# Turning the context of a cross-attention kernel on VectorE in 32x32 squares instead of on TensorE

## The reference

```
q = x @ Wq; k = ctx @ Wk; v = ctx @ Wv          # per head, 32 channels each
p = softmax(q @ k.T / sqrt(32))
out = merge_heads(p @ v) @ Wo + bias + x
```

## Time and profile before

| | |
|---|---|
| median of three runs | 1901.07 us |
| profiled execution | 1897.36 us, of which the span is 1895.7 us |
| TensorE busy | 1828.4 us (96%) |
| VectorE busy | 1184.8 us (63%) |
| ScalarE busy | 1044.8 us (55%) |
| GpSimd busy | 690.8 us (36%) |
| first phase, to TensorE's last matmul | about 316 us |
| second phase, from VectorE's first instruction | 326.4 us to the end |

### The profile page before, as it was taken

One profiled execution on the slowest core, in us unless ns is written; L12 is line 12 of the kernel. 1 busy time (PEld: TensorE's weight loads), 2 busy tenths in 40 slices (PEclk: granted clock), 3 DMA queues, 4 the chain that ended last, 5 costly groups with the idle time before them and its releaser, 6 DMA issues.

```text
span 1895.7 us, 41902 instructions
## 1 busy us (share of the span) xinstructions
PE 1828.4 (96%) x14960; PEld 1498.5 (79%) x14960; DVE 1184.8 (63%) x2402; ACT 1044.8 (55%) x5597; POOL 690.8 (36%) x865
## 2 busy tenths in 40 slices
PE   8999996789999999999999999999999999999998
PEld 7999996567777777777777777777777777777777
DVE  3201001677777777777777777777777777777762
ACT  4312111566666666666666666666666666666661
POOL 1111111244444444444444444444444444444441
PEclk9999998899999999999999999999999999999998
DMA  7522111688888888888888888888888888888873
GB/s 257 153 69 86 58 44 45 165 221 228 243 243 241 242 242 243 242 240 245 235 243 244 235 247 239 242 237 236 239 241 240 245 243 241 239 245 244 242 212 131
DMA packets 271397, 399.36 MB, mean 211 GB/s; under 512 B 41088, under 2 KB 119024, under 8 KB 271200
## 3 DMA queue, kind: packets, MB, share of 16 engines
q1 hardware_dynamic: 183008, 301.62, 54.2%
q10 hardware_dynamic: 83904, 82.59, 17.6%
q0 software_dynamic: 4288, 12.62, 1.9%
HBM read 216.37 MB, written 180.39 MB: 209 GB/s over the span
## 4 chain that ended last, share of the span: by engine, by line
PE 45%; DMA 22%; DVE 6%; ACT 5%; SPq 2%; issue 1%; POOL 1%; ACTq 0%; DVEq 0%
PE p_bank L776 21%; DMA p_scratch<-turned 15%; PE p_bank L735 14%; DMA probs_t<-p_scratch 7%; PE p_scores L750 5%; PE p_bank L762 5%; ACT probs L595 5%; DVE negmax L638 2%; SPq L508 2%; DVE turned L654 2%; DVE x_t L676 1%; POOL probs L562 1%; DVE x_bias L684 0%; DVE q_t L661 0%; DVE o_t L665 0%
## 5 line engine op out<-in xcount | busy, mean ns | idle before, releaser
L595 ACT ACTIVATE probs<-p_scores,negmax 128x77 f32<-128x77 f32 x2560 | 788.0, 362 | 550.4 <-DVE negmax L638 550.4
L562 POOL TENSOR_TENSOR probs<-probs,rsum 128x308 f32<-128x308 f32 x640 | 446.7, 700 | 895.6 <-DVE rsum L644 895.4
L776 PEld LDWEIGHTS p_bank<-wo_split,o_t 128*128 128x128 f32 x3840 | 567.6, 189 | 134.5 <-issue 131.3
L595 ACT ACTIVATION_READ_ACCUMULATOR probs<-p_scores,negmax 128x1 f32 x2560 | 624.5, 244 | 0.0
L776 PE MATMUL p_bank<-wo_split,o_t 128*128 128x320 f32 x3840 | 616.5, 315 | 0.6 <-DVE x_bias L684 0.6
L735 PE MATMUL p_bank<-x_t,wq_split 128*128 128x512 f32 x2400 | 597.1, 401 | 15.9 <-DVE x_t L676 15.9
L735 PEld LDWEIGHTS p_bank<-x_t,wq_split 128*128 128x128 f32 x2400 | 444.7, 190 | 115.4 <-DVE x_t L676 17.1
L654 DVE STREAM_TRANSPOSE turned<-probs 128x384 f32<-128x384 f32 x640 | 356.5, 557 | 29.2 <-POOL probs L562 28.8
L638 DVE TENSOR_REDUCE negmax<-p_scores 128x16 f32<-128x1232 f32 x160 | 229.3, 1433 | 48.0 <-PE p_scores L750 46.6
L644 DVE RECIPROCAL rsum<-sums 128x4 f32<-128x4 f32 x640 | 110.7, 173 | 178.6 <-ACT probs L595 174.1
L762 PE MATMUL p_bank<-probs_t,v_sb 77*32 77x512 f32 x1280 | 172.0, 609 | 26.9 <-DMA probs_t<-p_scratch 23.0
(11 more groups left out here) (28 smaller groups left out, 626.4 us busy)
## 6 DMA issues: line engine op xcount, KB each, us to landing
p_scratch<-turned SPq DMA_DIRECT2D x160, 768.0 KB, 6.8
probs_t<-p_scratch SPq DMA_DIRECT2D x320, 256.0 KB
x_bias<-in_x ACTq DMA_DIRECT2D x128, 320.0 KB, 3.7
out<-x_bias SPq DMA_DIRECT2D x128, 320.0 KB, 5.6
x_raw<-in_x ACTq DMA_DIRECT2D x124, 320.0 KB, 5.2
probs_t<-p_scratch SPq DMA_DIRECT2D x160, 104.0 KB
ctx_raw<-in_ctx SPq DMA_DIRECT2D x19, 512.0 KB, 4.7
k_sb<-k_scratch SPq DMA_DIRECT2D x32, 192.5 KB, 6.2
```

What stands on the lines that cost most here:

```text
L562: nc.gpsimd.tensor_tensor(heads_of(t), heads_of(t), rsum[:, slot, t, :].unsqueeze(2).to_broadcast([P, HG, N_TXT]), ALU.mult).then_inc(prob ...
L595: last = nc.scalar.activation(heads_of(t)[:, h, :], s_bank[:, h, t * N_TXT:(t + 1) * N_TXT], ACT.Exp, bias=negmax[:, slot, t, h:h + 1], ac ...
L776: last = nc.tensor.matmul(to_bank[:, 0:HALF], o_t[parity][:, o, c, t * P:(t + 1) * P], wo_s[:, w, c, hf * HALF:(hf + 1) * HALF], start=c = ...
```

## The change

The context is no longer turned by TensorE. SyncE loads a block in four transfers, one for each quarter of the channels (L189 of the new file): partition i * 32 + q of `ctx_raw` holds, for each of the eight groups n of 32 tokens, the 256 channels of quarter i of token n * 32 + q. Runs in memory are 256 floats instead of 1024. All four count on one semaphore for each half.

VectorE then transposes squares of 32x32 inside each group of 32 partitions (L292), 512 columns an instruction, into a new SBUF tile `ctx_turned` with two slots. ScalarE and VectorE read that in place of the PSUM bank for the high part (L251) and the low part (L298). The channels come out in another order: chunk k has channels i * 256 + k * 32 + s on partition i * 32 + s. Therefore the rows of wk and wv are loaded in that order too, by one transfer of a rearranged view for each chunk, and wq now likewise. The identity, its semaphores and two PSUM banks go.

`blocks` is a Python loop over all ten blocks; no engine has a hardware loop any more. `attend` is unchanged.

```diff
+CK = CA // (P // SQ)
...
-def blocks(eng, body):
-
-    for j in range(HEAD):
-        body(j, j % 2)
-    with eng.Fori(0, PAIRS) as i:
-        for half in range(2):
-            body(2 * i + (HEAD + half), (HEAD + half) % 2)
-    for j in TAIL:
+def blocks(body):
+
+    for j in range(BLOCKS):
         body(j, j % 2)
...
-            "ident": sbuf("ident", [P, P]),
-
...
-        ctx_raw = sbuf("ctx_raw", [P, CSLOTS, CA])
+        ctx_raw = sbuf("ctx_raw", [P, 2, TB // SQ, CK])
+        ctx_turned = sbuf("ctx_turned", [P, 2, 2, TB])
...
-        bank = [stack.enter_context(nc.psum_tensor(f"p1_bank{i}", [P, 512], F32)) for i in range(6)]
-        t_bank, k_bank, v_bank = bank[0:2], bank[2:4], bank[4:6]
-
-        id_zero, id_ready = sem("id_zero"), sem("id_ready")
+        bank = [stack.enter_context(nc.psum_tensor(f"p1_bank{i}", [P, 512], F32)) for i in range(4)]
+        k_bank, v_bank = bank[0:2], bank[2:4]
...
+        ctx_v = ctx.rearrange("(n q) (i c) -> i q n c", q=SQ, i=P // SQ)
...
-            def load_block(j, parity):
-                for i, (t0, rows) in enumerate(tiles_of(tokens_of(j))):
-                    slot = parity * CTILES + i
-                    if not isinstance(j, int) or j >= 2:
-
-                        sp.wait_ge(t_done, TU * (j - 1))
-                    sp.dma_start(ctx_raw[0:rows, slot, :], ctx[bass.ds(j * TB + t0, rows), :])\
-                      .then_inc(c_loaded[slot], DMA)
-
-            load_block(0, 0)
+            def load_block(j):
+                if j >= 2:
+                    sp.wait_ge(t_turned, TU * (j - 1))
+                n0, n1 = j * TB // SQ, (j * TB + tokens_of(j)) // SQ
+                for i in range(P // SQ):
+                    sp.dma_start(ctx_raw[i * SQ:(i + 1) * SQ, j % 2, 0:n1 - n0, :], ctx_v[i][:, n0:n1, :])\
+                      .then_inc(c_loaded[j % 2], DMA)
+
+            load_block(0)
             for n, (dram, _, k) in enumerate(chunks):
                 if n >= WSLOTS:
                     sp.wait_ge(w_split, n - WSLOTS + 1)
-                if dram is wq:
-                    for i in range(P // SQ):
-                        r = i * CQ + k * SQ
-                        sp.dma_start(stage[i * SQ:(i + 1) * SQ, n % WSLOTS, :], dram[r:r + SQ, :])\
-                          .then_inc(w_loaded[n % WSLOTS], DMA)
-                else:
-                    sp.dma_start(stage[:, n % WSLOTS, :], dram[k * P:(k + 1) * P, :])\
-                      .then_inc(w_loaded[n % WSLOTS], DMA)
+                rows = (dram[k * P:(k + 1) * P, :] if dram is wo else
+                        dram.rearrange("(i k s) c -> k i s c", i=P // SQ, s=SQ)[k])
+                sp.dma_start(stage[:, n % WSLOTS, :], rows).then_inc(w_loaded[n % WSLOTS], DMA)
...
@@ ScalarE
             def context_high(j, parity, u):
...
-                act.wait_ge(t_done, TU * j + u + 1)
+                act.wait_ge(t_turned, TU * j + u + 1)
                 nc.scalar.activation(ctx_t[parity][:, 0, 2 * u:2 * u + 2, 0:tokens],
-                                     t_bank[u % 2][:, 0:2 * tokens].rearrange("p (k t) -> p k t", k=2),
-                                     ACT.Copy).then_inc(t_high, 1)
+                                     ctx_turned[:, u % 2, :, 0:tokens], ACT.Copy).then_inc(t_high, 1)
...
@@ VectorE
+            def turn_context(j, parity, u):
+                n = tokens_of(j) // SQ
+                if u == 0:
+                    dve.wait_ge(c_loaded[parity], DMA * (P // SQ) * (j // 2 + 1))
+                if TU * j + u >= 2:
+                    dve.wait_ge(t_split, TU * j + u - 1)
+                blocks_in = ctx_raw[:, parity, 0:n, 2 * u * SQ:2 * (u + 1) * SQ]
+                nc.vector.transpose(ctx_turned[:, u % 2, :, 0:n * SQ].rearrange("p k (n q) -> p k n q", q=SQ),
+                                    blocks_in.rearrange("p n (k q) -> p k n q", q=SQ)).then_inc(t_turned, 1)
+
...
+            turn_context(0, 0, 0)
             for u in range(TU):
+                if u + 1 < TU:
+                    turn_context(0, 0, u + 1)
                 context_low(0, 0, u)
             split_weights(range(WK_CHUNKS))
 
             def body(j, parity):
                 for m in range(CC):
-                    if m < TU and not (isinstance(j, int) and j == BLOCKS - 1):
+                    if m < TU and j < BLOCKS - 1:
+                        turn_context(j + 1, 1 - parity, m)
                         context_low(j + 1, 1 - parity, m)
                     split_weights(splits_at(j, m))
...
@@ TensorE
-            def transposes(j, parity, u):
-                tokens = tokens_of(j)
-                if not isinstance(j, int) or TU * j + u >= 2:
-                    pe.wait_ge(t_split, TU * j + u - 1)
...
-            pe.wait_ge(id_ready, 1)
-            for u in range(TU):
-                transposes(0, 0, u)
-
             def body(j, parity):
                 for m in range(CC):
                     keys(j, parity, m)
-                    if m < TU and not (isinstance(j, int) and j == BLOCKS - 1):
-                        transposes(j + 1, 1 - parity, m)
                 values(j, parity)
```

More of the change, by code:

```diff
@@ L165, in loads_by @@
         def loads_by(n):
-            return sum(P // SQ if chunks[i][0] is wq else 1 for i in range(n % WSLOTS, n + 1, WSLOTS))
+            return n // WSLOTS + 1
+        ctx_v = ctx.rearrange("(n q) (i c) -> i q n c", q=SQ, i=P // SQ)
         def splits_at(j, m):
-            if not isinstance(j, int) or j >= HEAD:
+            if j >= HEAD:
                 return range(0)
@@ L220, in _ @@
                 sp.dma_start(kept["x_raw"][i * SQ:(i + 1) * SQ, 0, :, :], x_v[0][i]).then_inc(x_loaded, DMA)
-            with sp.Fori(0, PAIRS - 1) as i:
-                for half in range(2):
-                    load_block(2 * i + (4 + half), half)
-            for j in TAIL:
-                load_block(j, j % 2)
+            for j in range(4, BLOCKS):
+                load_block(j)
         @block.gpsimd
         def _(pool):
-            nc.gpsimd.memset(ident[:, :], 0.0).then_inc(id_zero, 1)
-            pool.wait_ge(id_zero, 1)
-            nc.gpsimd.affine_select(out=ident[:, :], in_=ident[:, :], compare_op=ALU.not_equal, fill=1.0,
-                                    base=0, pattern=[[-1, P]], channel_multiplier=1).then_inc(id_ready, 1)
             def store(j, parity):
@@ L270, in keys_out @@
                 act.wait_ge(k_done, CC * j + m + 1)
-                if not (isinstance(j, int) and CC * j + m < 2):
+                if not (CC * j + m < 2):
                     act.wait_ge(k_stored[slot], DMA // 2 * (CC * j + m - slot))
@@ L279, in values @@
                     act.wait_ge(v_done, VU * j + u + 1)
-                    if not (isinstance(j, int) and j == 0 and u < 2):
+                    if not (j == 0 and u < 2):
                         act.wait_ge(v_stored[u % 2], DMA * (VU // 2 * j + u // 2))
@@ L291, in body @@
                     keys_out(j, parity, m)
-                    if m < TU and not (isinstance(j, int) and j == BLOCKS - 1):
+                    if m < TU and not (j == BLOCKS - 1):
                         context_high(j + 1, 1 - parity, m)
@@ L295, in body @@
                 values(j)
-            blocks(act, body)
+            blocks(body)
         @block.vector
@@ L321, in body @@
                 for m in range(CC):
-                    if m < TU and not (isinstance(j, int) and j == BLOCKS - 1):
+                    if m < TU and j < BLOCKS - 1:
+                        turn_context(j + 1, 1 - parity, m)
                         context_low(j + 1, 1 - parity, m)
                     split_weights(splits_at(j, m))
-            blocks(dve, body)
+            blocks(body)
         @block.tensor
         def _(pe):
-            def transposes(j, parity, u):
-                tokens = tokens_of(j)
-                if not isinstance(j, int) or TU * j + u >= 2:
-                    pe.wait_ge(t_split, TU * j + u - 1)
-                for i, (t0, rows) in enumerate(tiles_of(tokens)):
-                    slot = parity * CTILES + i
-                    if u == 0:
-                        pe.wait_ge(c_loaded[slot], DMA // 2 * (j - parity) + DMA)
-                    for k in range(2):
-                        last = nc.tensor.transpose(t_bank[u % 2][:, k * tokens + t0:k * tokens + t0 + rows],
-                                                   ctx_raw[0:rows, slot, (2 * u + k) * P:(2 * u + k + 1) * P],
-                                                   ident[0:rows, 0:rows])
-                last.then_inc(t_done, 1)
             def keys(j, parity, m):
                 slot, tokens = (parity * CC + m) % 2, tokens_of(j)
-                if not (isinstance(j, int) and CC * j + m < 2):
+                if not (CC * j + m < 2):
                     pe.wait_ge(k_copied, CC * j + m - 1)
@@ L382, in body @@
                     keys(j, parity, m)
-                    if m < TU and not (isinstance(j, int) and j == BLOCKS - 1):
```

(3 more changed lines are left out.)

28 lines of the change are left out of this document (12 added, 16 removed).

## The result

The changed kernel takes 1932.46 us in the median (1930.7 to 1934.56, 4 runs), the kernel before 1900.92 (1899.89 to 1902.59, 4 runs): ratio 1.0165, 95% interval 1.0148 to 1.0183. It is 31.5 us slower where I forecast 10.3 us faster, and lies far outside the range. The profiled execution took 1934.56 us, its span is 1932.7.

A forecast was written before the change was run, and what follows sets the result against it. TensorE was taken to bound the first phase; -10.1 and -2.3 (transposes), +1.2 (start), +0.7 (block 0) and +0.2 (clock) sum to -10.3 us, so 1901.07 becomes 1890.8 us, range 1887.0 to 1897.0.

The forecast's parts named there:

- the sentence on the weights' loads: Start: weight loads of 320 KB, queued behind the context, land ahead of their use; no cost in the sum.
- Transposes, 12.4 us: TensorE, first phase: removing transposes saves 1.44 us in each of blocks 1 to 7 and 2.3 in block 8.
- Rival D: First phase: TensorE's matmuls don't close up where transposes stood, blocks stay at 30.2 us; 1903.2 us, 4%.
- Loops, 0: First phase: loop registers and branch cost TensorE nothing, so unrolling gains 0.
- Start, +1.2 us: Start: context lands at 7.0 us, then turns; first weight subtraction at 12.5 instead of 11.29 us.
- Rival A: Start: the context comes at full rate and the start costs next to nothing; -11.4 us, 1889.7 us, 15%.
- My line between rates by run length: Context load: between 640-byte and 4096-byte runs, 1024 bytes cost 56 ns, giving 291 GB/s and 3.6 us.
- the prediction's 3.4 us: Start: time by which the context load of before landed above its pure transfer time, carried over to the new load.
- Block 0's pace on VectorE, +0.7 us: Block 0: VectorE's order sets a 3.53 us period, TensorE waits 2.2 us; +0.7 instead of a 1.4 gain.
- the +0.2 for the clock: Start: TensorE's clock stays at 1.2 GHz a little past unit 0, so unit 1 pays; 0 to +0.5 us.
- Rival B: Block 0 or start: TensorE's wait or late start lowers its clock; +2.7 to +5.4, 1893.5 to 1896.2 us, 12%.
- Rival C: Second phase: moved addresses and timing add waits for probabilities through memory; 23 us longer, 1913.8 us, 6%; sign over 1572 us.

The follow-up runs named there:

- e1: Changed kernel with each weight chunk loaded as one plain piece of 128 rows, permutation left out; 1891.9 us, ratio 0.9964.
- e2: Changed kernel with the weight rows of a chunk taken in eight pieces of 16 rows, not matching the context's channels; 1909.2 us, ratio 1.0064.
- e4: Kernel before with only wk and wv loaded by the rearranged view in four pieces; 1939.9 us, ratio 1.0216.
- e8: Kernel before with the first phase written out without hardware loops, nothing else changed; 1900.2 us, ratio 1.0005.
- e5: Changed kernel with the same permuted weight rows, each chunk loaded by four transfers of 32 rows; 1896.4 us, ratio 0.9983.
- e6: Changed kernel with permuted wk and wv loaded by quarters of the channels, four chunks a transfer, wq by four transfers a chunk; 1903.1 us, ratio 1.0013.
- e12: Changed kernel with wk and wv rows at a stride of 8 over 128 partitions, VectorE's turns strided and one unit ahead, wq by four transfers; 1890.0 us, ratio 0.9949.
- e10: e1 with VectorE turning the context one unit ahead, in front of the weight subtractions; 1887.4 us, ratio 0.9939.
- e11: Changed kernel, turns one unit ahead, each wk and wv chunk in four 32-row transfers over the queues of SyncE, ScalarE and GpSimd; 1897.3 us, ratio 0.9989.
- e9: e6 with VectorE's turns one unit ahead and the identity's memory allocated again, unused; 1899.5 us, ratio 0.9998 to the kernel before.

## Why the prediction was wrong

**The step that failed** is the sentence on the weights' loads: "needed one in 0.75 us; they land one in 0.8 us from about 8 us on, ahead of their use". I took the rate of plain loads for the rearranged view. The view has four pieces outermost, runs on 4 of 16 engines, and lands a chunk in 3.19 us; that moved the start of the second phase by 39.3 us (e1), where the sum had nothing for it. The prediction named this load no further and had no rival for it: all my care with rates went to the context, where the order of instructions showed another shape, while `128x1x640` for the weights looked like the old `128x640`. The diff did show it: a slice of "(i k s) c -> k i s c" cannot be one dimension of 128. e1, e2 and e4 show the cause: 39 us in the changed kernel, 41 in the kernel before, halved engines and rates in step with the number of pieces.

**Transposes, 12.4 us**: right, a little small; 14.7 were won (7 x 1.73 + 2.6 in block 8). Rival D fell with that. A block lasts 28.47 us, not 28.76, since 120 matmuls in one piece run at 0.120 us each and not 0.1225: 1.73 a block instead of 1.44. The 390 ns for a transpose that the prediction quotes from the Trainium skill, "VectorE: DVE Perf Modes", section "The three transpose paths", stand there for bf16, and the context here is float32.

**Loops, 0**: right (e8).

**Start, +1.2 us**: the mechanism was right, the size small. VectorE begins at 7.73, not 7.0, and TensorE at 14.10 instead of 12.17, +1.9. Rival A, with a landing at 5.9, fell. From the landing to the first weight subtraction it is 5.49 us (7.73 to 13.22) where I had 5.5. My line between rates by run length was the wrong law: context (1024 bytes) at 223 to 234 GB/s in the changed kernel, x (640) at 218 to 251, weights (2560) in quarters at 241 in e5 are all alike and all go to 32 partitions a transfer. (The stages of x hold some other traffic too: of the 1.26 MB between 66.5 and 71.5 us 0.16 are stores, of the 1.31 between 329.5 and 335.5 us 0.47 came through another queue than x.) What the three have in common is the partitions, and the cleanest pair is e6 and e1, 225 against 394 GB/s from 10 to 12 us; e12 shows that the order of the rows in memory isn't it, since rows 8 apart come at 394. No run tried a number of partitions between 32 and 128. The Trainium skill, "SBUF — State Buffer", section "Door 1: The DMA port swizzle", says that 32 partitions reach 8 of 16 ports, about 218 GB/s. By it 1.05 MB take 4.8 us and, with the prediction's 3.4 us on top, land at 8.2, an estimate from that figure; they landed at 7.73. The stages measured here lie between 203 and 261 GB/s, so some are above it. By the rule that the prediction cites, 512 bytes for line rate in the Trainium skill, "DMA: Bandwidth & Descriptors", section "Specifications", runs of 1024 bytes would have come at full rate; they came at 223 to 234, so it is not what set the rate here.

**Block 0's pace on VectorE, +0.7 us**: the mechanism was right. The period was forecast at 3.53 and is 3.51, TensorE's wait 2.2 and 2.23 (e1), and the order was its cause (e10). The size was not: in e1 the values start 13.7 us after the first copy-out of keys (19.96 to 33.66), +0.4 and not +0.7, and that copy-out comes 0.4 us sooner after TensorE's start than before (5.8 instead of 6.2). Together nothing is left of the term. Nor of the +0.2 for the clock: the granted clock is 1.00 in e1's stages from 14 to 22 us. In the changed kernel itself the slower pace is hidden behind the loads.

**Rival B** (the clock falls in a wait) had no part with plain rows, where the value matmuls of block 0 take 14.34 us after a wait of 2.23. It was close: in e11 they take 15.88 after a wait of 2.25 us, and the granted clock fell there (columns as above).

```profile
38.00:40.00 2.00, 0.07 (x1) 0.07 (x1) 1.88 (x3) 0.32 (x1) 0.00 (x0) 1.00 1.14 223
40.00:42.00 2.00, 2.00 (x10) 2.00 (x11) 0.00 (x0) 0.00 (x0) 0.00 (x0) 0.64 1.08 284
```

In the changed kernel they take 16.55 after a wait of 10.72 us: the granted clock is 0.50 in the stages of 5 us before and after their start.

```profile
65.00:70.00 5.00, 0.00 (x0) 0.00 (x0) 0.99 (x2) 1.02 (x3) 0.00 (x0) 0.50 0.63 177
70.00:75.00 5.00, 4.29 (x16) 4.29 (x17) 0.66 (x1) 0.07 (x1) 0.54 (x1) 0.50 0.62 147
```

**Rival C** (the second phase): of the 31.5 us, 26.6 lie ahead of the second phase, and it lasts 1579.7 us in the profile against 1569.3, above the 1572 that I had named as this rival's sign. The place that I named has a part in it. TensorE's waits for the probabilities from memory, in all, times and longest, were 23.0, 32, 3.4 and are in the changed kernel

```profile
PE p_bank L732 <- DMA probs_t<-p_scratch: 29.3, 37, 3.3
```

6.3 of the 10.4 us. The reason isn't the addresses (e9). The waits go only roughly with the length: 22.0 us of them in e8 (1568.9 us) and 33.0 in e5 (1580.0), but 31.7 in e9 (1573.7). Over the profiles of the twelve other kernels the length goes from 1569 to 1580 us, and single runs of one kernel spread over up to 12 us (e8: 1893.7 to 1906.0). By medians, less the start of the second phase in the profile, the changed kernel, e1, e2 and e6, which turn the context behind the weights, have 1577 to 1580 us and the other kernels 1573 to 1576; but e5 has that order too and 1574. No run tests this lean. What lengthens the second phase stays open, and with it 5 us of the 31.5.

With plain rows the whole mechanism gives -12.7 us ahead of the second phase (-14.7 and +2.0) where I had -10.3. That e1 (1891.9) and e12 (1890.0) lie at the forecast of 1890.8 us is in part luck: e1 wins more than forecast in the first phase, and against the runs of the kernel before beside it (1899.1) it is only 7.2 us faster.

## What to carry to other kernels

Of every load that a change rewrites, write down its dimensions on both sides as the transfer carries them: in these runs the slowest one set how many DMA engines worked (4, 8 or 16), and whether a transfer covered 32 or 128 partitions set the rate of each. A permutation of rows written as one stride over 128 partitions loads as fast as plain rows (394 against 398 GB/s), and as a view in four pieces it costs three quarters of the bandwidth. The stride is not free where it is undone: here it made the turns slower, and the second phase 1.9 us later. When work moves to an engine that also has work to hand on, put the moved piece one unit ahead of what waits for it.

## What the runs showed of the hardware

- Transfers of the same 2560-byte rows: 97, 191 and 398 GB/s with 4, 8 and 128 as the outermost dimension of the source (changed kernel, e2, e1). SyncE's queue backs up behind slow ones: eight issues in 17.71 us instead of 3.90.
- 16 busy engines move 203 to 261 GB/s when each transfer ends in 32 partitions, whatever the run (640, 1024 or 2560 bytes), and whether one queue issues them or three (e5, e11).
- VectorE's 32x32 transpose of 128x512 takes 0.704 us from contiguous input and 1.135 us from every eighth element (32 bytes apart) (e10, e12).
- TensorE's granted clock stayed at 1.00 after a wait of 2.23 us in e1 and fell to 0.64 and then 0.50 after one of 2.25 us in e11, where the 96 value matmuls took 15.88 instead of 14.34 us.
